# Layer-norm means and variances computed by ScalarE accumulators instead of VectorE statistics, in an attention + RWKV kernel

## The reference, cut to what matters

```python
def _ln(x, w, b):
    m = jnp.mean(x, axis=-1, keepdims=True)
    v = jnp.mean((x - m) ** 2, axis=-1, keepdims=True)
    return (x - m) * jax.lax.rsqrt(v + EPS) * w + b
...
xn = _ln(x, ln1_w, ln1_b)
sx = _token_shift(xn, state[:, i1])
... # five mixes of xn and sx, projections r, k, v, g and the decay w
_, outs = jax.lax.scan(step, s0, xs)      # s = k v + w s, out = r (u k v + s)
... # group norm of the output, times the gate g
x = x + att * g @ Wo.T
xn2 = _ln(x, ln2_w, ln2_b)
... # squared-relu feed-forward with token shift
x = x + rr * (kk @ ffn_Wv.T)
```

## Time and profile before

| | us |
|---|---|
| median of 3 runs | 745.33 |
| lowest and highest | 740.27, 745.39 |
| the profiled execution | 745.93 |
| its span, first to last instruction | 743.7 |
| PE, DVE, ACT, POOL busy in the span | 661.4, 633.3, 366.4, 259.9 |
| mean granted TensorE clock | 0.959 |

### The profile page before, as it was taken

The page is one execution under the profiler, slowest core; times in us unless marked ns, Lnnn a source line. Parts: engine busy times, 40 slices in busy tenths (PEclk is TensorE's granted clock), DMA queues, the critical chain, the costliest instruction groups (busy, mean ns, idle before and its releaser), DMA issues.

```text
span 743.7 us, 9716 instructions
## 1 busy us (share of the span) xinstructions
PE 661.4 (89%) x2736; PEld 358.8 (48%) x2736; DVE 633.3 (85%) x989; ACT 366.4 (49%) x805; POOL 259.9 (35%) x186
## 2 busy tenths in 40 slices
PE   7689999988996869999999899899999989956996
PEld 5466666656442214453444435445344443523574
DVE  2499999994467899999999999999999999879623
ACT  3468888872242327446255444644625544352431
POOL 1850000001003674554536336355453633831000
PEclk9689999999998988999999999999999999986899
DMA  2611211110075146055152523705615232350000
GB/s 63 214 45 57 68 58 56 56 57 29 1 147 107 36 77 142 1 113 132 39 114 64 105 53 60 169 0 113 135 35 113 69 72 59 82 114 0 0 29 28
DMA packets 38298, 54.17 MB, mean 73 GB/s; under 512 B 4626, under 2 KB 21154, under 8 KB 38146
## 3 DMA queue, kind: packets, MB, share of 16 engines
q1 hardware_dynamic: 36866, 50.46, 30.3%
q0 software_dynamic: 1408, 3.43, 1.4%
HBM read 16.13 MB, written 4.19 MB: 27 GB/s over the span
## 4 chain that ended last, share of the span: by engine, by line
PE 28%; DVE 27%; issue 12%; ACT 4%; POOL 1%; DMA 1%; DVEq 1%; SPq 1%; ACTq 0%; POOLq 0%
DVE state L1295 10%; PE ps_a L794 5%; PE ps_a L765 4%; PE ps_c L853 3%; PE ps_c L867 3%; DVE x L1258 2%; DVE state L1282 2%; PE ps_att L833 2%; DVE st L1226 2%; PE ps_a L805 2%; PE ps_a L777 2%; PE ps_c L865 2%; PE ps_a L803 2%; PE ps_c L765 1%; DVE sx L1339 1%
## 5 line engine op out<-in xcount | busy, mean ns | idle before, releaser
L669 POOL TENSOR_TENSOR x<-x,xn 128x1024 f32<-128x1024 f32 x35 | 84.4, 2413 | 201.2 <-DVE x L1258 201.2
L1295 DVE TENSOR_TENSOR_SCAN state<-ps_w,state 128x512 f32<-128x512 f32 x128 | 145.8, 1198 | 0.7
L765 PE MATMUL ps_a<-x,wsq 128*128 128x512 f32 x256 | 117.9, 599 | 5.5 <-ACT xn L1033 3.0
L664 POOL TENSOR_TENSOR state<-vb,k 128x2016 f32<-128x2016 f32 x23 | 107.1, 4655 | 22.8 <-DMA vb<-v 16.0
L1300 DVE TENSOR_TENSOR vb<-state,r 128x2048 f32<-128x2048 f32 x32 | 95.4, 2981 | 1.6
L765 PEld LDWEIGHTS ps_a<-x,wsq 128*128 128x128 f32 x256 | 47.2, 191 | 65.6 <-issue 52.0
L1258 DVE SCALAR_TENSOR_TENSOR x<-ps_a,vec,sx 128x512 f32<-128x512 f32 x80 | 57.3, 742 | 14.2 <-PE ps_a L794 12.9
L794 PE MATMUL ps_a<-mix_t,w 128*128 128x512 f32 x128 | 62.5, 610 | 6.1 <-ACT mix_t L1038 6.1
L296 ACT ACTIVATE probs<-ps_f,negmax 128x256 f32<-128x256 f32 x128 | 58.9, 472 | 2.0 <-DVE negmax L345 1.2
L646 POOL TENSOR_TENSOR rs<-ve,mhalf 128x4 f32<-128x4 f32 x16 | 27.9, 1744 | 82.6 <-DVE ve L1232 82.6
L345 DVE TENSOR_REDUCE negmax<-ps_f 128x2 f32<-128x512 f32 x64 | 41.2, 685 | 7.5 <-PE ps_f L218 5.0
(11 more groups left out here) (170 smaller groups left out, 1258.1 us busy)
## 6 DMA issues: line engine op xcount, KB each, us to landing
vb<-v SPq DMA_DIRECT2D x128, 256.0 KB, 5.8
x<-in_x SPq DMA_DIRECT2D x32, 128.0 KB, 2.1
c<-in_ctx SPq DMA_DIRECT2D x32, 128.0 KB, 2.1
x_chunk<-in_x SPq DMA_DIRECT2D x8, 512.0 KB, 7.4
out<-sx SPq DMA_DIRECT2D x8, 512.0 KB, 3.5
wsq<-in_wsq POOLq DMA_DIRECT2D x1, 1024.0 KB, 5.2
wsq<-in_wsq POOLq DMA_DIRECT2D x1, 768.0 KB, 7.0
s<-in_s POOLq DMA_DIRECT2D x1, 512.0 KB, 7.9
```

The costliest lines, as they stand in the source:

```text
L664: nc.gpsimd.tensor_tensor(st[q][:, :, :, 1:L], src[:, :, :, 0:L - 1], wide(k[p][h][:, :])[:, :, :, 0:L - 1], ALU.mult).then_inc(kv_at(n, h ...
L669: nc.gpsimd.tensor_tensor(x5[j % 2][:, :, :], x5[j % 2][:, :, :], xn[:, :, 1:L1], ALU.add).then_inc(x5_ready, 1)
L765: mm = nc.tensor.matmul(bank[:, :], wsq[:, weight, c, P * o:P * o + P], src(c), start=(c == 0), stop=(c == EC - 1))
L1295: nc.vector.tensor_tensor_scan(row, w[h][:, :], row, 0.0, ALU.mult, ALU.add).then_inc(scanned, 1)
```

## The change

DVE no longer takes the moments of either layer norm, except for chunk 0 of layer norm 1. ACT does it in four passes more. For layer norm 1 a new step `a_zs` copies each of the four 128x256 tiles of z into `zn` (which serves as scratch) with an accumulator that sums the row, turns the four sums into negated means with one 128x4 activation, then `deviations` squares z minus the mean tile by tile with a second accumulator, and one 128x4 activation makes the variance plus eps. For layer norm 2 the copy out of PSUM is split from two 128x512 into four 128x256 activations that sum as they copy, and a new step `c_xs` does the rest. Both write the same `ve` tiles that POOL's `rstd` reads, and count up the same semaphores.

```diff
+            def deviations(n, veb, scratch, s_var, s_sq, sq_at):
+
+                act.wait_ge(s_var, n * 2 + 1)
+                if not isinstance(n, int):
+                    nc.scalar.copy(apart[:, :], eps[:, 0:1])
+                for m in range(TILES):
+                    nc.scalar.activation(scratch[:, E * m:E * m + E], wyz[:, bass.ds(n * TILES + m, 1), :].rearrange("p a f -> p (a f)"), ACT.Square,
+                                         bias=veb[:, 1, m:m + 1], accum_out=row_sq[:, m:m + 1]).then_inc(s_sq, 1)
+                act.wait_ge(s_sq, sq_at)
+                nc.scalar.activation(veb[:, 0, :], row_sq[:, :], ACT.Identity, bias=eps[:, 0:1], scale=1.0 / E).then_inc(s_var, 1)
+
+            def a_zs(n):
+                act.wait_ge(z_ready, n + 1)
+                if not isinstance(n, int):
+                    nc.scalar.copy(apart[:, :], eps[:, 0:1])
+                for m in range(TILES):
+                    nc.scalar.activation(zn[:, E * m:E * m + E], wyz[:, bass.ds(n * TILES + m, 1), :].rearrange("p a f -> p (a f)"), ACT.Copy,
+                                         accum_out=row_sum[:, m:m + 1]).then_inc(row_sums1, 1)
+                act.wait_ge(row_sums1, (n - 1) * TILES + TILES)
+                nc.scalar.activation(ve1[:, 1, :], row_sum[:, :], ACT.Copy, scale=-1.0 / E).then_inc(ln1_var, 1)
+                deviations(n, ve1, zn, ln1_var, row_sqs1, (n - 1) * TILES + TILES)
...
             def c_x1(n):
                 for i in range(2):
                     act.wait_ge(c_done, c_at(n, f"o{i}"))
-                    nc.scalar.activation(wyz[:, bass.ds(n * TILES + 2 * i, 2), :], cb(f"o{i}")[:, :].rearrange("p (m f) -> p m f", m=2),
-                                         ACT.Copy).then_inc(x1_ready, 1)
+                    for m in range(2):
+                        mm = nc.scalar.activation(wyz[:, bass.ds(n * TILES + 2 * i + m, 1), :].rearrange("p a f -> p (a f)"),
+                                                  cb(f"o{i}")[:, E * m:E * m + E], ACT.Copy, accum_out=row_sum[:, 2 * i + m:2 * i + m + 1])
+                    mm.then_inc(x1_ready, 1)
+
+            def c_xs(n):
+                act.wait_ge(x1_ready, n * 2 + 2)
+                nc.scalar.activation(ve2[:, 1, :], row_sum[:, :], ACT.Copy, scale=-1.0 / E).then_inc(ln2_var, 1)
+                deviations(n, ve2, zn2, ln2_var, row_sqs2, n * TILES + TILES)
...
                 state_column(n, 1, 0)
                 c_x1(n - 1)
+                c_xs(n - 1)
                 state_column(n, 1, 1)
...
                 c_square(n, 0)
                 if z:
+                    a_zs(n + 2)
+                if z:
                     a_norm(n + 2)
                 a_copy(n + 1, "r", r[q], r_ready)
...
                 a_mod(n + 1, 1)
-                c_x1(n - 1)
                 a_mod(n + 1, 2)
...
                 a_mod(n + 1, 3)
-                if z:
-                    a_zm(n + 2)
                 b_kv(n, p, 1, 1)
```

More of the change, by code:

```diff
@@ L493, in rwkv @@
     c_done = sem("c_matmuls_done")
+    row_sums1, row_sqs1, row_sums2, row_sqs2 = sem("ln1_row_sums"), sem("ln1_row_squares"), sem("ln2_row_sums"), sem("ln2_row_squares")
     init_done, low_zero = sem("init_done"), sem("low_rows_zeroed")
@@ L532, in rwkv @@
         eps, apart = sb("eps", [P, 2]), sb("apart", [P, 1])
+        row_sum, row_sq = sb("row_sum", [P, TILES]), sb("row_sq", [P, TILES])
         zn = sb("zn", [P, TILES * E])
```

## The result

The changed kernel takes 755.59 us (median of 4 runs, 752.70 to 760.51), the kernel before beside it 744.15 (740.27 to 745.39): a ratio of 1.0175, interval 1.0136 to 1.0214. The ratios are taken over the fast executions of a series and differ a little from the quotient of the two medians (1.0154 here). By the medians the loss is 11.4 us in the first series and 13.2 in the second. The profiled execution took 760.51 us, its span is 758.4, so 14.7 us more than the span before; it is the slowest of its four, which is why the spans differ by more than the medians.

A forecast was written before the change was run, and what follows sets the result against it. It took DVE's work up to xm, with PE close behind, as the bound. Bodies 16.0, drain 1.0 and last pass 0.5 sum to 17.5 us on 745.93: 763, own range 752 to 774, overall 750 to 786.

The forecast's parts named there:

- a_zs, 4.7 us: ACT's layer norm 1 statistics in a body take 4.7 us, so the variance is there at 459.9.
- The power held up by c_final until 461.6: POOL's power in a body waits for DVE's c_final, ending 0.87 us after it, at 461.6.
- The prediction's own branch without the hold-up: If c_final doesn't hold up POOL's power, a body comes out 2.6 us longer, 13 us in all.
- DVE's wait, 5.9 us: Behind c_final DVE waits 5.9 us for POOL's product k v; the scans start at 466.6 instead of 465.29.
- The product with r, 4.2 us: DVE's product after the scans takes 4.2 us instead of 2.29 alone, beside POOL's second product k v, until 475.4.
- The body, +3.2 us: Each of bodies 1 to 5 lasts 3.2 us longer because xm and PE's mix come later; 16.0 us in all.
- Layer norm 2 free in the bodies: ACT's layer norm 2 statistics cost 0 in the bodies, with 0.7 us of cover ahead of the state column.
- Drain +1.0: In drain_pass nothing covers layer norm 2; second copy to normalising takes 5.1 us instead of 4.13, +1.0 (0 to 3).
- Last pass +0.5: In last_pass layer norm 2 costs the same as in drain_pass, but half lies behind the scans: +0.5 us.
- its sum by the rule, 16 us: By the shared-port rule POOL's power waits for c_final, making a body 3.2 us longer, 16 us in all.
- Rival 1: TensorE's clock falls in each body behind PE's longer waits: +3 us a body, 15 more, 778 us; chance 0.17.
- Rival 2: Faster: variance ready early enough, by short a_zs or another place in ACT's time, PE bounds; 740 us; chance 0.09.

The follow-up runs named there:

- e3: The changed kernel with a_zs moved earlier in ACT's body, ahead of c_rr instead of behind c_square, same instructions; 738.43 us, ratio 0.991.
- e5b: The changed kernel with the four accumulating copies of a_zs made twice at the same place; 770.59 us, ratio 1.0353.
- e8: The changed kernel with the product k v of part (0, 0) on DVE behind c_final instead of on POOL; 743.92 us, ratio 1.0002.
- e1: The changed kernel with layer norm 1's moments back on DVE, layer norm 2 staying on ACT; 746.88 us, ratio 1.0033.
- e12: The changed kernel, unaltered, measured once more in a second series; 756.22 us, ratio 1.017.
- e7: The kernel before with layer norm 1's moments left out of bodies 1 to 5, results wrong, only time of use; 740.71 us, ratio 0.998.
- e2: The changed kernel with layer norm 2's moments back on DVE, layer norm 1 staying on ACT; 757.34 us, ratio 1.0125.
- e10: e3 measured once more, on another series' chip; 741.53 us, ratio 0.995.

## Why the prediction was right, and where it was off

**The direction and the chain were right.** 763 was forecast, with slower at 0.83; 755.59 came, inside the range. Of the 17.5 us forecast 14.7 came in the profiled execution and 11.4 by the medians. In part the 14.7 are luck: the bodies gave 4.4 us less than forecast, and the end stretch 3.1 instead of 1.5. Each link of the chain is in the trace: ACT's variance late, POOL's two products k v behind it, DVE waiting at the scan of (0, 0), its product stretched, xm and PE's mix late, in bodies 1 to 5 and not in 6. e3, e5b and e8 show that this chain is the cause.

- **a_zs, 4.7 us:** 4.56. Four copies step by 0.40 us, four squares by 0.49, where the attention's row gave 0.46 for both.
- **The power held up by c_final until 461.6, the mis-sized step:** it is held up by 0.1 us and not by 0.7. It took 1.11 us instead of 1.01 and ended at 530.12, less 69.26 at 460.9. The two halves of c_final were priced as one operation. They are two: the first ended at 529.25 (528.57 + 0.68), the power ended 0.87 after that, the very figure used in the prediction, and the second half held up nothing. The product k v so ended at 465.7 (534.93 less 69.26) and not at 466.6; 0.7 us of that is the hold-up, the rest the hand-overs. The prediction's own branch without the hold-up, 2.6 us a body and 13 in all, was nearer.
- **DVE's wait, 5.9 us:** 5.16, and the scans at 465.75 instead of 466.6, by the same 0.85.
- **The product with r, 4.2 us:** 3.96; the overlap came out at 1.8 us (539.68 to 541.49) instead of 2.1, since POOL's second product ended at 472.2 and not at 473.3.
- **The body, +3.2 us:** +2.3 (64.0 to 64.3 against 61.7 to 61.9), 11.6 over five instead of 16.0. Nearly all of the difference, 0.85 us, is the scans' earlier start that follows from the misjudged hold-up.
- **Layer norm 2 free in the bodies:** right (e1: bodies of 61.7 to 61.9).
- **Drain +1.0:** from the second copy to the normalising 4.91 us (730.43 to 735.34) instead of 4.13, +0.8.
- **Last pass +0.5:** too low in the profiled execution. It went from 4.12 to 6.39 there, of which 1.5 is one POOL product behind DVE's product with r:

```profile
690.92 1.01 POOL L648 TENSOR_TENSOR rs<-ve,mhalf 128x4 f32<-128x4 f32 x1 [12.71 <-ACT ve L1034]
692.01 1.67 POOL L650 TENSOR_TENSOR rs<-ve,rs 128x4 f32<-128x4 f32 x1
```

  That is a matter of where the passes fall: in e12, the same kernel, `L650` took 0.20 there, the normalising came 4.92 us after the copy, and the end stretch lasted 76.5 us instead of 79.1. What makes up the rest of these 2.6 us is open.

The Trainium skill's rule (SBUF — State Buffer, "Who interferes with whom") says that whoever of VectorE and GpSimd issues first holds the shared port for the whole instruction. The trace agrees where a product, an add_x or a half of c_final is ahead, once it is applied to single instructions: a DVE product with r ended 2.15 us after POOL's product three times (before, after, e7). It doesn't agree where POOL's small power is ahead. In after the second half of c_final took its 0.69 us alone beside it (529.17 to 529.86, the power until 530.12), and in e3 the product with r starts 0.4 us before the power's end and isn't held up at all, while the bias product behind the power (`L650`, 0.20 us alone) is held up by it in turn:

```profile
450.89 1.01 POOL L648 TENSOR_TENSOR rs<-ve,mhalf 128x4 f32<-128x4 f32 x1 [2.04 <-ACT ve L1034]
451.99 1.91 POOL L650 TENSOR_TENSOR rs<-ve,rs 128x4 f32<-128x4 f32 x1
```

```profile
451.54 2.29 DVE L1338 TENSOR_TENSOR vb<-state,r 128x2048 f32<-128x2048 f32 x1
```

The prediction had applied the rule to the pair of c_final's halves, and its sum by the rule, 16 us, was therefore not what the rule gives.

**Rival 1, the clock falls in bodies (0.17),** is half true. In the profiled execution of after it stayed at 1.00 in bodies 1 to 5. In e12, the same kernel, it fell in two of the five: to a mean of 0.97 in the first, which lasted 64.5 us, and of 0.92 in the third, which lasted 67.89. Busy time by stretch of that body, and PE's timeline at its end:

```profile
419.24:487.13 67.89, 62.11 (x193) 29.41 (x192) 55.66 (x53) 38.05 (x90) 31.71 (x16) 0.92 0.36 77
```

```profile
475.01 2.42 PE L827 MATMUL ps_a<-bonus,cst 128*128 128x512 f32 x4 [1.91 <-DVE bonus L1307]
478.18 3.78 PE L779 MATMUL ps_a<-zn,w 128*128 128x512 f32 x4 [0.75 <-DVE zn L1287]
482.64 3.78 PE L796 MATMUL ps_a<-mix_t,w 128*128 128x512 f32 x4 [0.69 <-ACT mix_t L1062]
```

Two of the groups of products take 3.78 us, nearly twice their 1.98, at 1.2 GHz. The price is 3.7 us in this body, near the rival's 3, and 0.3 in the first: it wasn't paid five times. e2 had the same in the same two bodies. The wait alone doesn't decide it: the clock fell in e12 behind waits of 1.90 and 1.91 us for r u k, and after has 1.90, 1.90 and 1.91 in three of its bodies and kept it. In e5b, with waits of 2.6 to 3.0 ahead of the gate projection, the mean was below 1.00 in all five.

**Rival 2, faster at another place of ACT's list,** named e3: 740 was worked out, 738.4 and 741.5 were measured. Its reason was too generous (6 x 1.2; a body gave 0.77): what is late next, here ACT's mix_t, takes most of it (0.88 of 1.19).

**What the prediction didn't see** is why DVE, 99% busy, isn't worth its time. It took PE as the reason. e7 shows another for the moments of layer norm 1: DVE's busy time contains a hold-up by POOL that grows to fill what is saved.

## What to carry to other kernels

Before work is moved off a full engine, look for who consumes the result and what is queued behind that consumer: here 4.6 us at a late place of an engine that is idle 40% of the time cost 2.3 us a body, and the same instructions four steps earlier in its list cost nothing. A busy share may be inflated by operations that stand waiting for another engine inside their own duration; compare each with its shortest instance (2.29 against 3.68 or 6.00) before counting it as work. Price such a hold-up instruction by instruction, from the end of the one that holds.

## What the runs showed of the hardware that was not expected

- A reduction by ACT's accumulator is cheap: with plain copies from SBUF of 128x256 the starts step by 0.40 us, with a square and a bias from SBUF by 0.49, with copies out of PSUM by 0.37 (684.34 and 684.71 in after's last pass); the reading of the accumulator, 0.19, lies inside that step.
- A held-up operation ends at the end of the one that holds it plus its own duration alone less 0.14 us: 2.15 us for the product with r (2.29 alone), 0.87 for the power (1.01), 0.56 for the second half of c_final (0.69 alone; in before it ended at 465.37, POOL's add_x at 464.81). A small operation ahead doesn't hold up one behind it: the power of 128x4 left c_final's half and the product with r at their 0.69 and 2.29 us.
- The spread of a kernel's runs arises early. e3 and e10 are one kernel; their spans are 738.9 and 730.7 us, and the first (0, 1) scan of the bodies starts at 295.37 and 287.05: the whole difference of 8.2 us lies ahead of it, and between 20 and 40 us the granted clock was 0.67 in the one and 0.91 in the other. The busy time by stretch of e3, then of e10:

```profile
20.00:40.00 20.00, 14.39 (x72) 9.43 (x72) 9.39 (x25) 9.24 (x32) 17.23 (x34) 0.67 0.60 189
```

```profile
20.00:40.00 20.00, 15.97 (x113) 10.35 (x109) 15.08 (x39) 13.11 (x43) 17.66 (x36) 0.91 0.66 215
```

  What sets it there wasn't tried.
